# A decoder layer in three steps: attention loops written out, softmax sums and norms taken once for four heads

## The reference

```python
x = x + attn(layernorm(x), Wq, Wk, Wv, Wo)      # B=2, T=512, D=1024, 32 heads of 32, 8 key/value heads, rotary, causal
x = x + fake_quant(layernorm(x)) @ fake_quant(ctx)   # ctx 1024 x 1024 for each batch, 8 bit
x = x + fixed_point(layernorm(x), weight, bias)      # Q8.8 integers, 1024 x 1024
```

```python
q = (x @ Wq).reshape(b, t, 32, 32).transpose(0, 2, 1, 3)     # k and v alike, with 8 heads
q, k = rope(q), rope(k)
scores = einsum('bhqd,bhkd->bhqk', q, repeat(k, 4)) / sqrt(32), causal mask
ctx = einsum('bhqk,bhkd->bhqd', softmax(scores), repeat(v, 4))
out = ctx.transpose(0, 2, 1, 3).reshape(b, t, 1024) @ Wo
```

## Time and profile before

| | |
|---|---|
| median of 3 runs | 586.71 us (585.56 to 589.8) |
| profiled execution, its time | 589.05 us |
| profiled execution, its span | 587.2 us |
| granted TensorE clock, mean | 0.952 |

### The profile page before, as it was taken

One profiled execution on the slowest core, in us unless ns is written; L12 is line 12 of the kernel. 1 busy time (PEld: TensorE's weight loads), 2 busy tenths in 40 slices (PEclk: granted clock), 3 DMA queues, 4 the chain that ended last, 5 costly groups with the idle time before them and its releaser, 6 DMA issues.

```text
span 587.2 us, 12002 instructions
## 1 busy us (share of the span) xinstructions
PE 492.4 (84%) x4050; PEld 279.8 (48%) x4050; DVE 394.1 (67%) x763; ACT 327.5 (56%) x395; POOL 259.5 (44%) x242
## 2 busy tenths in 40 slices
PE   2678998587689889898899999999798999976776
PEld 2356643233355555455565555555443444444333
DVE  5875277464587788787866877887439466767436
ACT  2654233200577766677757888888943531456533
POOL 5030113324367779767784555456652734230000
PEclk9898998779999999999969999999999899987899
DMA  9821366522301110011103222112355110000015
GB/s 313 255 86 59 115 178 173 148 88 89 90 2 47 45 45 18 29 44 45 48 22 133 91 93 90 39 52 91 109 204 220 42 36 19 1 2 1 33 42 215
DMA packets 42616, 50.68 MB, mean 86 GB/s; under 512 B 4049, under 2 KB 32337, under 8 KB 42577
## 3 DMA queue, kind: packets, MB, share of 16 engines
q1 hardware_dynamic: 25792, 41.69, 21.3%
q10 hardware_dynamic: 16784, 8.46, 5.0%
HBM read 40.57 MB, written 9.44 MB: 85 GB/s over the span
## 4 chain that ended last, share of the span: by engine, by line
PE 37%; DVE 19%; DMA 12%; issue 11%; POOL 10%; ACT 7%; SPq 3%; DVEq 0%; ACTq 0%; POOLq 0%
PE ps L1352 10%; DMA rope_scratch<-s1reg 7%; PE ps L1457 4%; PE ps L1220 4%; DVE stat L725 4%; PE ps L1179 3%; PE ps L1414 3%; DMA qstack<-rope_scratch 3%; POOL s1reg L1092 3%; PE ps L1240 2%; PE ps L1207 2%; DVE mt L781 2%; PE ps L1255 2%; POOL wkv L1100 2%; POOL s1reg L1111 2%
## 5 line engine op out<-in xcount | busy, mean ns | idle before, releaser
L781 DVE TENSOR_REDUCE mt<-ps 128x1 f32<-128x512 f32 (+3 forms) x256 | 113.2, 484 | 50.3 <-PE ps L1222 47.9
L1179 PE MATMUL ps<-xT,wqx 128*128 128x512 f16 x384 | 99.3, 397 | 3.9 <-DVE s1reg L772 3.5
L1352 PE MATMUL ps<-wo_reg,xT 128*128 128x512 f16 x384 | 94.2, 384 | 2.3 <-DVE wqx L813 2.2
L1111 POOL TENSOR_TENSOR s1reg<-s1reg 128x1280 f16<-128x1280 f32 x32 | 83.7, 2614 | 28.1 <-ACT s1reg L510 26.5
L503 ACT ACTIVATE s1reg<-ps 128x1280 f32<-128x1280 f32 x64 | 78.9, 1233 | 24.4 <-PE ps L1242 22.5
L1220 PE MATMUL ps<-kreg,qstack 96*128 (+4 forms) x256 | 72.4, 314 | 22.1 <-DVE mt L781 15.3
L510 ACT ACTIVATE s1reg<-s1reg 128x1280 f16<-128x1280 f32 x64 | 81.3, 1270 | 2.8
L1240 PE MATMUL ps<-qstack,kreg 98*128 (+4 forms) x256 | 58.0, 303 | 11.8 <-DMA qstack<-mrow 8.3
L797 DVE TENSOR_TENSOR s1reg<-s1reg 128x1280 f16<-128x1280 f32 x32 | 53.3, 1667 | 15.1 <-ACT s1reg L510 15.1
L1100 POOL TENSOR_TENSOR wkv<-wkv 128x128 f32<-128x128 f32 x64 | 35.1, 549 | 62.4 <-DVE rcp L803 62.3
L1179 PEld LDWEIGHTS ps<-xT,wqx 128*128 128x128 f16 (+1 forms) x384 | 35.6, 102 | 43.7 <-issue 13.8
(11 more groups left out here) (123 smaller groups left out, 790.0 us busy)
## 6 DMA issues: line engine op xcount, KB each, us to landing
s1reg<-in_ctx SPq DMA_DIRECT2D x16, 512.0 KB, 4.6
qstack<-rope_scratch SPq DMA_DIRECT2D x48, 128.0 KB, 2.4
rope_scratch<-s1reg SPq DMA_DIRECT2D x40, 128.0 KB
qstack<-in_x SPq DMA_DIRECT2D x8, 512.0 KB, 5.3
s1reg<-in_L_attn_Wq ACTq DMA_DIRECT2D x8, 512.0 KB, 4.8
s1reg<-in_L_attn_Wo ACTq DMA_DIRECT2D x8, 512.0 KB, 5.3
s1reg<-in_x SPq DMA_DIRECT2D x16, 256.0 KB, 2.9
out<-s1reg SPq DMA_DIRECT2D x7, 512.0 KB, 2.7
```

The costliest lines, as they stand in the source:

```text
L781: nc.vector.reduce_max(mt[:, 2 * hp + e, qt:qt + 1], ps[:, 3 + e, 0:P * (qt + 1)], AX.X).then_inc(s_max, 1)
L1111: nc.gpsimd.tensor_tensor(pl[:, j % 2, :], ebuf[:, j % 2, :], ph[:, j % 2, :], ALU.subtract).then_inc(pl_done[1], 1)
L1179: last = mm(out_ap, w(ws, k), xT[:, xs, KT * b + k, :], start=(k == 0 and n == 0), stop=(k == KT - 1 and n == 2))
L1352: last = mm(ps[:, bank, :], xT[:, os, KT * b + k, t], wo_sb[:, ws, 4 * h:4 * h + 4, k, :], start=(k == 0 and n == 0), stop=(k == KT - 1 an ...
```

## The change

The two loops are replaced by Python loops: every group is written out, with constants in place of registers. `pvs` has four buffers and `osum` four parts. The reciprocals, sums and norms are taken once for a group (`inverse_sums`, `heads_out`), all four heads in one instruction each, after head 3's copy, at the place where head 3's were taken before. The copies to `pvs` wait for the sums and reciprocals of the group before. The low part of head 2 in batch 1 goes from VectorE to GpSimd. The semaphores of the low parts are one for each head instead of two.

```diff
-        def attention_c(eng, body):
-            body(0, 0, False, True)
-            with eng.Fori(1, KV - 1) as g:
-                body(g, g, True, True)
-            body(KV - 1, KV - 1, True, True)
...
+        def attention_c(body):
+            for g in range(KV):
+                body(g, g, g > 0, True)
+
+        def attention_d(body):
+            for g in range(KV):
+                body(KV + g, g, True, g < KV - 1, g // 2, g % 2)
...
             def pv_out(G, j):
                 act.wait_ge(pv_done, G * 4 + (j + 1))
-                if not (isinstance(G, int) and G == 0 and j < 2):
-                    act.wait_ge(o_norm, G * 4 + (j - 1))
-                nc.scalar.activation(pvs[:, j % 2, :, :], ps[:, PV, 0:TT * VW].rearrange("p (t c) -> p t c", t=TT),
+                if G:
+                    act.wait_ge(den_done, G)
+                    act.wait_ge(o_sum, G)
+                nc.scalar.activation(pvs[:, j, :, :], ps[:, PV, 0:TT * VW].rearrange("p (t c) -> p t c", t=TT),
                                      ACT.Copy).then_inc(pvs_done, 1)
...
-            def inverse_sum(G, j):
-                dve.wait_ge(pvs_done, G * 4 + (j + 1))
-                if not (isinstance(G, int) and G == 0 and j < 2):
-                    dve.wait_ge(o_norm, G * 4 + (j - 1))
-                nc.vector.reciprocal(rcp[:, j % 2, :], pvs[:, j % 2, :, 2 * DH]).then_inc(den_done, 1)
+            def inverse_sums(G):
+                dve.wait_ge(pvs_done, G * 4 + 4)
+                if G:
+                    dve.wait_ge(o_norm, G)
+                nc.vector.reciprocal(rcp[:, :, :], pvs[:, :, :, 2 * DH]).then_inc(den_done, 1)
...
                 if tail:
-                    inverse_sum(G - 1, 3)
+                    inverse_sums(G - 1)
                 ahead_max(2, 3)
                 ahead_max(4)
-                inverse_sum(G, 0)
                 ahead_max(5)
...
                 if ahead:
                     split_max(G + 1)
-                p_low(G, 2)
-                inverse_sum(G, 1)
+                if G < KV:
+                    p_low(G, 2)
                 late()
                 if context:
                     dve.wait_ge(st_done, G * 4)
                     ctx(g * 2 - 2, 0)
                     ctx(g * 2 - 1, 1)
-                inverse_sum(G, 2)
...
-            def head_out(G, j):
-                pool.wait_ge(den_done, G * 4 + (j + 1))
...
-                nc.gpsimd.tensor_tensor(osum, pvs[:, j % 2, :, 0:DH], pvs[:, j % 2, :, DH:2 * DH], ALU.add).then_inc(o_sum, 1)
...
+            def heads_out(G):
+                pool.wait_ge(pvs_done, G * 4 + 4)
+                nc.gpsimd.tensor_tensor(osum, pvs[:, :, :, 0:DH], pvs[:, :, :, DH:2 * DH], ALU.add).then_inc(o_sum, 1)
+                pool.wait_ge(o_sum, G + 1)
+                pool.wait_ge(den_done, G + 1)
+                if G:
                     pool.wait_ge(ot_done, G)
-                nc.gpsimd.tensor_tensor(ogrp[:, :, DH * j:DH * j + DH], osum,
-                                        rcp[:, j % 2, :].unsqueeze(2).broadcast_to([P, TT, DH]), ALU.mult).then_inc(o_norm, 1)
+                nc.gpsimd.tensor_tensor(ogrp[:, :, :].rearrange("p t (j c) -> p j t c", j=HG), osum,
+                                        rcp[:, :, :].unsqueeze(3).broadcast_to([P, HG, TT, DH]), ALU.mult).then_inc(o_norm, 1)
...
             def body(G, g, tail, ahead, p=None, u=None):
                 if tail:
-                    head_out(G - 1, 3)
+                    heads_out(G - 1)
                 p_low(G, 1)
-                head_out(G, 0)
-                head_out(G, 1)
+                if p is not None:
+                    p_low(G, 2)
                 p_low(G, 3)
-                head_out(G, 2)
                 if p is None:
                     rotated(G + 12)
```

More of the change, by code:

```diff
@@ L124, in build @@
         ogrp = wkvf[:, 0:512].rearrange("p (t c) -> p t c", t=TT)
-        osum = wkvf[:, 512:640].rearrange("p (t c) -> p t c", t=TT)
-        pvs = wkvf[:, 640:640 + 2 * TT * VW].rearrange("p (s t c) -> p s t c", s=2, t=TT)
+        osum = wkvf[:, 512:1024].rearrange("p (j t c) -> p j t c", j=HG, t=TT)
+        pvs = wkvf[:, 1792:1792 + HG * TT * VW].rearrange("p (j t c) -> p j t c", j=HG, t=TT)
         ctx_st = s1reg[:, 5120:7168].rearrange("p (s n) -> p s n", s=2)
@@ L181, in build @@
         st_done, e_done, ph_done = sem("st_done"), sem("e_done"), sem("ph_done")
-        pl_done = [sem("pl_even"), sem("pl_odd")]
+        pl_done = [sem(f"pl_done{j}") for j in range(HG)]
         pv_done, pvs_done, den_done = sem("pv_done"), sem("pvs_done"), sem("den_done")
@@ L500, in exp @@
                 act.wait_ge(st_done, G * 4 + (j + 1))
-                if not (isinstance(G, int) and G == 0 and j < 2):
-                    act.wait_ge(*pl_count(G, j))
+                if not (G == 0 and j < 2):
+                    low, before = pl_count(G, j - 2) if j >= 2 else pl_count(G - 1, j + 2)
+                    act.wait_ge(low, before + 1)
                 nc.scalar.activation(ebuf[:, j % 2, :], st_ps[:, 0:SCORES], ACT.Exp, scale=EXP_SCALE,
@@ L794, in p_low @@
                 dve.wait_ge(ph_done, G * 4 + (j + 1))
-                if not (isinstance(G, int) and G == 0 and j < 2):
+                if not (G == 0 and j < 2):
                     dve.wait_ge(pv_done, G * 4 + (j - 1))
-                nc.vector.tensor_tensor(pl[:, j % 2, :], ebuf[:, j % 2, :], ph[:, j % 2, :], ALU.subtract).then_inc(pl_done[0], 1)
-            def inverse_sum(G, j):
-                dve.wait_ge(pvs_done, G * 4 + (j + 1))
-                if not (isinstance(G, int) and G == 0 and j < 2):
-                    dve.wait_ge(o_norm, G * 4 + (j - 1))
-                nc.vector.reciprocal(rcp[:, j % 2, :], pvs[:, j % 2, :, 2 * DH]).then_inc(den_done, 1)
+                nc.vector.tensor_tensor(pl[:, j % 2, :], ebuf[:, j % 2, :], ph[:, j % 2, :], ALU.subtract).then_inc(pl_done[j], 1)
+            def inverse_sums(G):
[3 more added lines that the diff above has]
+                nc.vector.reciprocal(rcp[:, :, :], pvs[:, :, :, 2 * DH]).then_inc(den_done, 1)
             def ot_low(G):
@@ L1094, in rotated @@
                 nc.gpsimd.tensor_tensor(xhl[:, 1, :], rx, xhl[:, 0, :], ALU.subtract).then_inc(rope_lo, 1)
-            def head_out(G, j):
-                pool.wait_ge(den_done, G * 4 + (j + 1))
-                if not (isinstance(G, int) and G == 0 and j == 0):
-                    pool.wait_ge(o_norm, G * 4 + j)
-                nc.gpsimd.tensor_tensor(osum, pvs[:, j % 2, :, 0:DH], pvs[:, j % 2, :, DH:2 * DH], ALU.add).then_inc(o_sum, 1)
-                pool.wait_ge(o_sum, G * 4 + (j + 1))
-                if j == 0 and not (isinstance(G, int) and G == 0):
+            def heads_out(G):
[4 more added lines that the diff above has]
+                if G:
@@ L1108, in p_low @@
                 pool.wait_ge(ph_done, G * 4 + (j + 1))
-                if not (isinstance(G, int) and G == 0 and j < 2):
+                if not (G == 0 and j < 2):
                     pool.wait_ge(pv_done, G * 4 + (j - 1))
-                nc.gpsimd.tensor_tensor(pl[:, j % 2, :], ebuf[:, j % 2, :], ph[:, j % 2, :], ALU.subtract).then_inc(pl_done[1], 1)
+                nc.gpsimd.tensor_tensor(pl[:, j % 2, :], ebuf[:, j % 2, :], ph[:, j % 2, :], ALU.subtract).then_inc(pl_done[j], 1)
             def body(G, g, tail, ahead, p=None, u=None):
@@ L1129, in _ @@
+            attention_d(body)
+            heads_out(NG - 1)
             steps = [0]
@@ L1248, in values @@
                 pe.wait_ge(low, before + 1)
-                if not (isinstance(G, int) and G == 0 and j == 0):
+                if G or j:
                     pe.wait_ge(pvs_done, G * 4 + j)
```

36 lines of the change are left out of this document (13 added, 23 removed).

## The result

The changed kernel takes 595.09 us, the median of five runs (593.75 to 598.44), against 586.71 for the kernel before: a ratio of 1.0123 [1.0085, 1.0161]. It is slower by 1.2%, some 7 us. The forecast was 590.7, in the range and on the right side of zero, but its terms are off in both directions and partly cancel, as the stretches show: that it came this near is in part luck.

The account below looks back on a forecast made before the run. Batch 0 was taken as bound by a 17.7 us ring of GpSimd, TensorE, VectorE and ScalarE, batch 1 by TensorE. 2.7 - 0.7 + 3.0 - 1.0 = +4.0 us gave 590.7 us, range 582 to 599 (8 of 10).

Parts of the forecast that it names:

- the ring: Batch 0: chain from GpSimd's norm through TensorE's output transpose to the next low part of head 3, 17.7 us a group.
- 2.46 us for the pair: Batch 0, GpSimd: one sum and one norm over all four heads, 512 elements a partition, bounds 1.0 and 5.0 us.
- The late DMA vanishes from the ring: Batch 0: rotated queries are written 0.9 us sooner, so TensorE no longer waits for a late row-maxima DMA.
- the two long steps: Batch 0: two of seven group steps took 18.8 us, 1.1 us more, put down to the maxima DMA ending late.
- I take 0.1 us for six edges of batch 0 and 0.2 for two of batch 1: Loops written out: registers and branches go, -1.0 us, bounds 0 and -3.
- the +2.7: Batch 0: seven steps of 18.4 us with four heads' sums and norms at once, 128.8 against 126.1 us.
- The third rival: Branches were dearer than seen: leaving each loop costs a stretch like ScalarE's 1.1 us wait; 587.5 us, chance 0.05.
- +3.0 us: Batch 1: VectorE's first conversion delays GpSimd's low part of head 2, and TensorE, by 0.5 us in six groups.
- Group 8 has no conversions and waits for the maxima DMA: Start of batch 1: moving head 2's low part to GpSimd was counted as 0 in group 8.
- -0.7 us: Change of batch: the maxima DMA's path shortens by 0.9 us, 0.84 usable by TensorE, other waits eating a little.
- The first rival: Batch 0 falls to the pace of batch 1, its seven steps taking 117.6 us; 579.5 us, chance 0.2.
- The second rival: VectorE and GpSimd obstruct each other: batch 1 loses 8.4 us instead of 3.0, batch 0 2.1 more; 598.2 us, chance 0.25.

Follow-up runs that it names:

- two pairs: Kernel before with loops written out and sums and norms taken for two heads at once, low parts divided as before: 584.94 us, 0.9939.
- the late transpose: Kernel before with loops written out and TensorE's output transpose about 3 us later in each group of batch 0: 585.74 us, 0.9926.
- conversions late: Changed kernel with VectorE's context conversions in batch 1 waiting until GpSimd's low part of head 2 is done: 594.76 us, 1.0111.
- the wait in group 8: Changed kernel; in group 8 alone GpSimd's low part of head 2 waits until VectorE has split the maxima: 591.68 us, 1.0035.
- only group 8 filled: Changed kernel with eight extra unused matmuls ahead of the one output transpose that runs in group 8: 593.0 us, 1.0062.
- all waits filled: Changed kernel with eight extra unused matmuls on TensorE ahead of each output transpose's wait for the norm in batch 0: 587.41 us, 0.998.

## Why the prediction was right and where it was wrong

**Right.** The side, and the mechanism of the loss in batch 0: GpSimd's pair in the ring through the output transpose. "2.46 us for the pair" measured 2.36, and "The ring becomes 18.4 us" measured 18.17, in every step at full clock. "The late DMA vanishes from the ring" held: with the loops alone TensorE still waits 4.2 us for it in seven places, in the changed kernel 0.9 once. But the two long steps, which the term counted with it, went with the loops. The lock of a whole instruction held in the meetings shown here (2.58 and 2.62 for 0.17, 2.85 for 2.62, 3.00 for 2.62, 2.27 for 1.49): each time the second was held for what the first had left, less some 0.14 us. That the whole came within 4.4 us is partly luck: by the stretches batch 1 came out 3.0 us below the forecast, and the long steps of batch 0 and the change of batch 3.8 and 5.5 above it.

**"I take 0.1 us for six edges of batch 0 and 0.2 for two of batch 1", "Bounds: 0 and -3."** Mis-sized. The term measured -4.4 us by the medians and -3.8 by the ratio, with the bound of -3 inside the interval; by the stretches it is 2.9 in the steps of batch 0, 1.1 at the change of batch (where the clock differs too) and 1.4 in batch 1. I had looked for gaps at the loop's edges on TensorE. "SP needs about 0.1 us less per DMA, which lies in slack after the change above" was the place: SP's path to the maxima DMA became 0.8 us shorter in each group of batch 0, and ahead of the two long steps it was not slack. Their 2.2 us stood in the sum already, in the +2.7, under the pair's name; beyond them the loops gave 0.7 in batch 0. In batch 1 four steps became 0.3 to 0.5 shorter. The third rival had this size (3.2 us more than the forecast, so -4.2), and I gave it 0.05. Its mechanism, a long fetch at each branch, is not what was seen: no stretch of one us without a releaser went from TensorE's path.

**"+3.0 us" for the third low part.** Right mechanism, half the size: 0.25 in place of 0.5 a group, in five groups in place of six, with 1.5 us for the stretch. The first conversion started 0.38 us before the low part, which left 0.37 of its 0.75, and the low part was held for 0.23.

**"Group 8 has no conversions and waits for the maxima DMA ... so both count 0", and "-0.7 us" for the change of batch.** This is the step that failed. Moving head 2's low part to GpSimd there cost 3 to 4 us (23.6 to 24.0 with the split blocked, 19.5 to 20.8 with it free, both at a lower clock), and the change of batch went from 19.1 to 24.0 us. I had looked in group 8 for the victim I knew, the conversions, and had not asked what else VectorE has to do under that low part. The lock has another victim there: the small second split of the maxima, in front of TensorE's transpose.

**"A wait of TensorE's output transpose for GpSimd of about 0.9 us in each group."** It is 1.7 us in the steps of batch 0 and 2.3 in group 8, and I gave it no consequence but its own length. The longer ring was not the only price: in some steps the granted clock falls, and such a step costs 1.2 to 1.7 us more. With that wait filled no such step was seen, and the collision of group 8 was gone with them.

**The sum by measured stretches:** loops -5.4 (2.9 + 1.1 + 1.4); on top of them the pair +4.0, one to three long steps +1.5 to +3.8, the change of batch +5.6 to +5.9 (23.7 or 24.0 for 18.0), and batch 1 +0.4 to +1.1 (third low part +1.3 to +1.9, packed heads -0.8). That is +6.1 to +9.4 us. The ratios of the two comparisons give 6.4 and 7.2, the profiled execution 9.4.

The first rival asked for a pair of under 1.5 us and falls with its 2.36. The second rival (598.2, the engines get in each other's way) was closer in time than the forecast, by 3.1 us against 4.4, and right in kind but not by its own places: neither the second conversion nor a longer ring in batch 0 did it. The part of the change that costs nothing is the loops written out alone, at 0.9936; what was tried on top of it (0.9939 with two pairs, 0.9926 with the late transpose) can't be told from it.

## What to carry to other kernels

When an operation moves to GpSimd, list all that VectorE may start while it runs, the smallest first: a 0.17 us instruction in front of a TensorE wait can cost the whole length of GpSimd's. Fewer and larger instructions help only where their starts are on the path; packed at the end of a ring, the four heads' work waits for the last head. And a new wait of TensorE has two prices, its length and the granted clock behind it; matmuls that do nothing are a quick test of which one is paid.

## What was not expected of the hardware

- An instruction of VectorE on 128x16 elements, with both operands in SBUF, took 2.58 to 2.62 us in three profiles beside a low part of GpSimd, and 0.17 or 0.18 when it started before (311.45, 311.17). The Trainium skill, SBUF — State Buffer, "SBUF: two separate sides", has it that an operation of VectorE with two SBUF inputs contends for the lock against a GpSimd operation that reads SBUF; by that rule the trace agrees.
- TensorE's granted clock: seven profiles have this longer wait (1.7 us) unfilled in the seven steps of batch 0 (the changed kernel twice, low part on VectorE in all groups or in group 8, conversions late, the wait in group 8, only group 8 filled). Of these 49 steps 11, in five of the profiles, were 19.4 to 19.8 us and the rest 18.2; the windows above show 0.91 and 1.00 for one of each. With all waits filled it was none of 7, and none of 21 in the three kernels with single heads or two pairs. Why one step falls to the 1.2 GHz level for a while and the next does not is open. The Trainium skill, TensorE: Matmul & The Clock Gate, "HAM oscillation — how this bites in real kernels", tells of a kernel whose waits between its matmuls bring the lower clock again and again. Its waits are longer than these, and 38 of the 49 steps here kept the full clock, so the trace agrees in kind only.
- Sizes on GpSimd, f32: an addition of 128, 256 and 512 elements a partition took 0.46, 0.73 and 1.28 us; the product with a broadcast reciprocal 0.40, 0.62 and 1.05.
